# VectorE normalises q directly behind k, and SyncE fetches the next layer's up weights right behind the last up product

## The reference

```
qkv = shift(x) @ Wqkv                        # 128 -> 3 x 1024, 16 heads of 64
q, k = l2norm(q) * q_scale, l2norm(k) * k_scale   # per token and head
q, k = rotary(q), rotary(k)                  # x*cos + rotate_half(x)*sin
p = softmax(q k^T over a window of own and previous 32 tokens)
x = (p v) @ Wo + x
xn = layernorm(shift(x));  a, gate = split(xn @ W1 + b1)     # 128 -> 2 x 341
x = (a * gelu(gate)) @ W2 + b2 + x
```

## Time and profile before

| | |
|---|---|
| median of 3 runs | 2389.36 us (2389.02 to 2389.78) |
| profiled execution, time | 2393.62 us |
| profiled execution, span | 2391.5 us |
| busy: PE / DVE / ACT / POOL | 79% / 58% / 55% / 62% of the span |
| mean granted TensorE clock | 0.942 of full speed |
| chain that ended last | PE 70%, DVE 22%, issue 5% |

### The profile page before, as it was taken

The page is one execution under the profiler, slowest core; times in us unless marked ns, Lnnn a source line. Parts: engine busy times, 40 slices in busy tenths (PEclk is TensorE's granted clock), DMA queues, the critical chain, the costliest instruction groups (busy, mean ns, idle before and its releaser), DMA issues.

```text
span 2391.5 us, 48609 instructions
## 1 busy us (share of the span) xinstructions
PE 1890.1 (79%) x18100; PEld 1165.2 (49%) x18100; DVE 1382.1 (58%) x2779; ACT 1311.1 (55%) x2363; POOL 1483.4 (62%) x1200
## 2 busy tenths in 40 slices
PE   6678888788787788788788778888878888777887
PEld 4345554445454444454445444545544454444554
DVE  3555665655565655556656555566655665646564
ACT  2355655655456556455565555565645655646553
POOL 2577676666566666566666656666656676656660
PEclk7699999989899999999999989999989999989998
DMA  3022222222222222222212121222221221111221
GB/s 82 18 55 60 53 52 51 47 54 52 54 47 52 51 52 52 51 52 55 46 44 66 45 55 45 52 48 56 54 56 43 52 53 42 45 46 44 45 50 36
DMA packets 154989, 120.46 MB, mean 50 GB/s; under 512 B 42577, under 2 KB 151173, under 8 KB 154629
## 3 DMA queue, kind: packets, MB, share of 16 engines
q1 hardware_dynamic: 154757, 117.35, 21.0%
HBM read 18.66 MB, written 1.05 MB: 8 GB/s over the span
## 4 chain that ended last, share of the span: by engine, by line
PE 70%; DVE 22%; issue 5%; SPq 1%; DMA 1%; ACT 0%; POOL 0%; DVEq 0%; ACTq 0%; POOLq 0%
PE qk_bank L366 18%; PE ring_bank L436 9%; PE ring_bank L377 7%; PE ring_bank L460 7%; PE sc_bank L411 7%; PE ring_bank L504 5%; DVE qkn L841 5%; DVE ss L807 5%; PE ring_bank L424 4%; PE ring_bank L449 3%; PE ring_bank L398 3%; PE ring_bank L515 3%; DVE uT L939 2%; DVE o L881 1%; PE ring_bank L495 1%
## 5 line engine op out<-in xcount | busy, mean ns | idle before, releaser
L1029 POOL TENSOR_TENSOR turned<-qkn,tables 128x512 f32<-128x512 f32 x384 | 488.2, 1271 | 759.3 <-DVE qkn L833 447.3
L366 PE MATMUL qk_bank<-wqkv,xT 128*128 128x512 f32 x768 | 442.2, 705 | 381.6 <-DVE qkn L841 381.6
L617 ACT ACTIVATE vs<-ring_bank 128x512 f32<-128x512 f32 x192 | 114.6, 597 | 793.2 <-PE ring_bank L377 793.2
L881 DVE TENSOR_TENSOR o<-ring_bank,rr 128x512 f32<-128x512 f32 x192 | 132.8, 692 | 687.3 <-PE ring_bank L436 687.3
L1036 POOL TENSOR_TENSOR turned<-qkn,tables 128x512 f32<-128x512 f32 x384 | 488.6, 1272 | 0.0
L366 PEld LDWEIGHTS qk_bank<-wqkv,xT 128*128 128x128 f32 x768 | 147.1, 213 | 535.1 <-DVE qkn L841 374.4
L644 ACT ACTIVATE kB<-ring_bank 64x512 f32<-64x512 f32 x384 | 225.2, 586 | 74.8 <-PE ring_bank L398 72.5
L1072 POOL TENSOR_TENSOR turned<-turned 128x512 f32<-128x512 f32 x192 | 243.6, 1269 | 15.1
L1065 POOL TENSOR_TENSOR turned<-turned 128x512 f32<-128x512 f32 x192 | 243.2, 1267 | 15.1
L436 PEld LDWEIGHTS ring_bank<-vw,pT 128*32 128x32 f32 x6144 | 164.4, 114 | 171.9 <-issue 170.3
L377 PE MATMUL ring_bank<-wqkv,xT 128*128 128x512 f32 x384 | 217.6, 648 | 36.1 <-DVE uT L939 34.6
(11 more groups left out here) (155 smaller groups left out, 2907.2 us busy)
## 6 DMA issues: line engine op xcount, KB each, us to landing
vw<-vs SPq DMA_DIRECT2D x1152, 64.0 KB, 2.1
vw<-vs SPq DMA_DIRECT2D x672, 32.0 KB, 1.9
wqkv<-in_L_ffn_Wqkv_dram SPq DMA_DIRECT2D x20, 384.0 KB, 3.5
wo<-in_L_ffn_Wo_dram SPq DMA_DIRECT2D x20, 128.0 KB, 3.2
w<-in_L_ffn_W_dram SPq DMA_DIRECT2D x6, 341.0 KB, 3.4
wqkv<-in_L_ffn_Wqkv_dram SPq DMA_DIRECT2D x1, 1536.0 KB, 10.6
x<-in_x_dram SPq DMA_DIRECT2D x2, 512.0 KB, 4.2
out_dram<-x SPq DMA_DIRECT2D x4, 256.0 KB, 2.5
```

The source lines that it names most:

```text
L366: mm = pe.matmul(QK[u % 2][:, i * UW:(i + 1) * UW], tok, wqkv[:, layer % 2, cut:cut + UW], start=True, stop=True)
L1029: return pool.tensor_tensor(heads(turned[:, u % 2, 2 * i, :]), heads(qkn[:, u % 2, i * UW:(i + 1) * UW]), table.unsqueeze(1).to_broadcast( ...
```

## The change

Nothing is added or removed; four things stand elsewhere.

1. DVE's scale_q(n-2) moves from behind clamp_squares to directly behind scale_k(n-2), ahead of maxima.
2. PE's fold_bias moves from s = 0 to s = 2, and DVE's add_bias from s = 1 to s = 3.
3. SP's fetch of W1 becomes next_up(g-2) at s = 6, with its wait for the last a product of the layer.
4. SP's fetch of W2 stays at s = 0 of the following group as next_down(g-3), with its wait for the down product.

```diff
@@ PE
                 if s == 0:
+                    mean(g - 2)
+                if s == 2:
                     fold_bias(g - 2)
-                    mean(g - 2)
@@ DVE
                 scale_k(n - 2)
+                scale_q(n - 2)
                 maxima(n - 4)
                 invert_sum(n - 5)
                 less_maxima(n - 4)
                 if s == 1:
-                    add_bias(g - 2)
                     centre(g - 2)
                 if s == 2:
                     add_eps(g - 2)
+                if s == 3:
+                    add_bias(g - 2)
...
-                scale_q(n - 2)
                 scale_o(n - 5)
@@ SP
-            def next_ffn(g):
+            def next_up(g):
                 if not 0 <= g < GROUPS - B or g % B != B - 1:
                     return
-                layer = g // B + 1
                 sp.wait_ge(*evicted("a1", g))
-                sp.dma_start(w1[:, 0:2 * DFF], W1[layer]).then_inc(w1_dma, 16)
+                sp.dma_start(w1[:, 0:2 * DFF], W1[g // B + 1]).then_inc(w1_dma, 16)
+
+            def next_down(g):
+                if not 0 <= g < GROUPS - B or g % B != B - 1:
+                    return
                 sp.wait_ge(*evicted("down", g))
-                second_weights(layer)
+                second_weights(g // B + 1)
...
+                if s == 6:
+                    next_up(g - 2)
                 if s == 0:
-                    next_ffn(g - 3)
+                    next_down(g - 3)
```

## The result

| | before | after |
|---|---|---|
| median of 4 runs | 2389.57 us | 1880.76 us (1878.25 to 1884.01) |
| ratio after / before | | 0.787, 95% interval 0.785 to 0.789 |
| span of the profiled execution | 2391.5 us | 1879.4 us |
| mean granted TensorE clock | 0.942 | 0.98 |

The change takes 509 us off, 21%. The forecast was 1945 us, with a range of 1850 to 2040; the time lies in the range, 64 us under the forecast and 11 us from the first rival (PE alone bounds it, 1870). It lies outside the 1895 to 1995 that the prediction gave its likeliest case.

The account below looks back on a forecast made before the run. A loop through DVE between attend and the q and k product bounds the kernel. Afterwards 86.0 + 133 + 1581 (21 x 75.3) + 5 + 66 + 77 give a span of 1948, say 1945 us; range 1850 to 2040.

Parts of the forecast that it names:

- the first rival: PE alone bounds the kernel, port collisions all fall into slack: 72.2 us a group, 1870 us; chance 0.25.
- likeliest case: DVE and POOL port collisions delay PE in short slots: 75.3 us a group, 1895 to 1995 us; chance 0.46.
- the signs that the prediction named: Qkn wait a tenth, no L476 DMA wait, fold groups alike, 75 us groups, newton above 0.18, POOL 75% busy, L504 wait.
- The bound: DVE loop between attend and q and k product; scale_q's 381.6 us wait nearly goes, PE work 70.7 us a group.
- The up weights: PE's wait for w1's DMA at the fold: all 10.8 us go, five times, 54 us.
- What falls later: On DVE, maxima, less_maxima, mask and exponentials come 0.61 us later; over 2 us of slack, so costed at nothing.
- DVE against POOL: Shared SBUF port blocks newton, clamp_squares and rstd_newton in short slots; PE waits 3.1 us a group.
- The hand walk: One group traced with blocked DVE steps: PE loses 0.6 at s = 1, 2.2 at s = 3, 0.3 at s = 5.
- The first two groups: Little PE work, so POOL sets the pace at 8.7 us a unit: 62 + 71 = 133 us.
- The sum: All parts of the span together: 1948 us, 443 under the span of 2391.5; forecast time 1945.
- The copies of v: Rival: copies of v land too late for ACT, 0.5 us in four slots of 24 groups, 1995 us; chance 0.04.
- The slower case: Rival: path over maxima, mask and scores ends last, takes 0.61 in each of 192 slots, 2452 us; chance 0.02.

## Why the prediction was right, and where it was off

The mechanism was right and the range holds the time, but the range does so because it was stretched over most of the first rival: 1881 lies 14 us outside the 1895 to 1995 of the case that had the highest chance. One term was too large, the cost of the collisions, 3.1 us a group forecast and 0.7 measured. Of the signs that the prediction named, a group of 75 us and PE's first L504 waiting for xnT failed (72.3 us; 7.3 us of waits in all, 6.9 before); the others came.

- *The bound.* Right: a loop over DVE between attend and the q and k product, and moving scale_q takes it off the path. This alone gives 1933. The 70.7 us of PE work in a group were 69.9, 0.8 too many: a short slot is 7.55, not 7.64. This is 17 us in 21 groups.
- *The up weights.* Right in mechanism: 5 waits of 7.0 and the clock behind them, 52 us with scale_q moved against 54 forecast less 5 for the folds' own work. That both the fetch and the fold had to move was never said, and they had not. fold costs its 1.1 in six groups.
- *What falls later.* Right: maxima, less_maxima and the mask 0.6 later cost nothing that shows; PE waits for no mask: its scores stand idle for 0.3 us in all.
- *DVE against POOL.* The mechanism was right and its size wrong. The collisions are in the trace, 230 us of DVE time, and POOL on half of the heads takes them away. But the term of 3.1 us a group (0.6 at s = 1, 2.2 at s = 3, 0.3 at s = 5) was 0.7 (about 0.4, 0.3 and nothing, and 0.1 at s = 2). The hand walk that gave it put newton and scale_k behind the whole of POOL's unit. At s = 1 of the group shown POOL ends 3.5 behind attend, as in the walk, but by then two steps are done and the blocked third ends with it, so scale_k ends 4.3 behind attend where I had 4.7. At s = 2 one step is blocked, the next starts before POOL's next instruction, and scale_k ends 3.9 behind attend, ahead of POOL's 4.2, where I had 5.5. By s = 3 the differences had added up: scale_o is 1.3 late, not 3.2, and the slot loses 0.3, not 2.2. The 2.4 a group are 50 us of the forecast.
- *The first two groups.* POOL sets the pace in the first, as forecast, and in short slots of the second, but at 7.6 to 7.8 a unit, not 8.7. 122 against 133 us. With POOL on half of the heads the second group isn't shorter (65.5 against 64.7).
- *The sum.* Span 1948 forecast, 1879.4 measured: 60 from the 21 groups, 11 from the first two, half a microsecond from the last, less 2 in the tail. The 17 and 50 us above are 67; a sixth fold and small waits give 7 of them back. That the likeliest case should have been the first rival comes from the one term. That rival was right by luck in part: its 72.2 a group has 0.8 too much work for PE and nothing for the collisions, which cost 0.7, and its premise, that POOL ends just ahead of newton and nothing collides, is wrong (160 of 192 units have a blocked step).
- *The rule of the Trainium skill* (SBUF — State Buffer, "Who interferes with whom") agrees with the traces after: steps of 0.17 us take up to 1.2 beside a POOL instruction, and the second one is back at 0.177 on average with POOL's halved. It says who is blocked, and for how long; it doesn't say what it costs the kernel. That was a question of slack, and there the walk erred.
- *The other rivals.* The copies of v: ACT waited 19.6 us for their DMA, in 22 waits, and PE not at all for it. The slower case did not come.

What stays open: why the lower clock level falls on the slots that it does when PE idles a little in each, and so why the fetch and the fold gave 33 us with scale_q at its old place, and why the kernel before gained only 12 us from POOL on half.

## What to carry to other kernels

In a pipeline across engines that runs in order, put first on the engine in between what the bounding engine waits for, and behind it what only other stages need: one line, moved up past five instructions, gave 456 of the 509 us.

When such a loop opens, engines that took turns start to overlap; look at what they share, but price a collision by the slack of the path it lies on, not by how often it occurs. 230 us of blocked DVE time cost 14 us in the 21 groups here. With the next wait removed, they took back 0.7 of the 1.6 us that its slot had gained.

For a fetch that comes too late, moving its consumer by two slots did as much as moving the fetch (1882 and 1885 us).

## What the runs showed of the hardware

- Two long DVE and POOL instructions can delay each other in turn: after the change rstd_newton's second instruction takes 1.57 us on average instead of 0.69, and POOL's beside it took 1.73 instead of 1.27 in the group shown.
- Behind a DVE instruction that waited for POOL's to end, the next small one passed too: it was ready 0.03 us later and started 0.02 us ahead of POOL's next instruction.
- Even clamp_squares, one SBUF input of 16 columns, is blocked by POOL: 0.65 us on average, 0.17 at least.
- With gated moved and POOL on half of the heads, PE ran 69.9 us of a group without a gap at the full clock (PEclk 1.00).
